# First norm of a two-layer graph kernel: its positive part made from a second, feature-major layout of x instead of by transposes

## Reference, cut to what matters

```python
h = maximum(layernorm(x), 0)
W = zeros(1024, 1024).at[src, dst].add(edge_weight)      # edge weights scattered into a dense matrix
x = x + h @ W.T + bias
h = maximum(layernorm(x), 0)
for layer in (0, 1):                                      # two graph layers with weights Ws, Wn of 1024 x 1024
    agg = segment_sum(h[src], dst) / degree
    h = h @ Ws + agg @ Wn + b                             # relu after layer 0
x = x + h
```

## Time and profile before

| | us |
|---|---|
| median of 3 runs | 824.98 (823.58 to 825.27) |
| the profiled execution, own time | 826.84 |
| its span | 825.1 |
| TensorE (PE) matmul busy in it | 798.2 (97%) |
| VectorE (DVE) busy | 469.8 (57%) |
| GpSimd (POOL) busy | 384.3 (47%) |
| ScalarE (ACT) busy | 378.3 (46%) |
| mean granted TensorE clock | 0.998 of full |

### The profile page before, as it was taken

The page is one execution under the profiler, slowest core; times in us unless marked ns, Lnnn a source line. Parts: engine busy times, 40 slices in busy tenths (PEclk is TensorE's granted clock), DMA queues, the critical chain, the costliest instruction groups (busy, mean ns, idle before and its releaser), DMA issues.

```text
span 825.1 us, 13564 instructions
## 1 busy us (share of the span) xinstructions
PE 798.2 (97%) x4660; PEld 647.1 (78%) x4661; DVE 469.8 (57%) x799; ACT 378.3 (46%) x491; POOL 384.3 (47%) x558
## 2 busy tenths in 40 slices
PE   3999999999999999999999999999999999999998
PEld 2666788888888878887887878888877888878786
DVE  7999666657542677856623453232556757336443
ACT  6755653443354222222336876543222333257653
POOL 3000056556735688756661210114788676724311
PEclk9999999999999999999999999999999999999999
DMA  3122335565464863556865653555753669758654
GB/s 108 43 69 82 99 116 177 172 182 170 159 234 159 275 207 105 181 202 216 319 219 180 196 175 102 179 175 178 268 170 116 196 212 332 253 180 281 209 170 138
DMA packets 82520, 148.57 MB, mean 180 GB/s; under 512 B 9973, under 2 KB 21356, under 8 KB 82448
## 3 DMA queue, kind: packets, MB, share of 16 engines
q1 hardware_dynamic: 62506, 102.68, 39.2%
q10 hardware_dynamic: 18422, 40.05, 13.7%
q0 software_dynamic: 1520, 4.92, 1.5%
HBM read 100.34 MB, written 47.27 MB: 179 GB/s over the span
## 4 chain that ended last, share of the span: by engine, by line
PE 73%; POOL 8%; issue 5%; DMA 4%; DVE 4%; ACT 4%; SPq 1%; ACTq 0%; POOLq 0%; DVEq 0%
PE bank L1306 28%; PE bank L1334 19%; PE bank L1243 13%; POOL T L848 3%; PE bank L1161 3%; PE bank L1150 3%; DMA stage<-hT_scratch 3%; PE bank L1166 2%; POOL T L846 2%; ACT split L1009 1%; PE bank L1145 1%; POOL S L817 1%; POOL S L813 1%; ACT Ax L1041 1%; PE bank L1350 1%
## 5 line engine op out<-in xcount | busy, mean ns | idle before, releaser
L1306 PE MATMUL bank<-slot,split 128*128 128x512 f32 x1680 | 388.6, 392 | 2.9 <-POOL split L831 1.2
L1306 PEld LDWEIGHTS bank<-slot,split 128*128 128x128 f32 x1680 | 314.5, 188 | 71.6 <-issue 3.0
L793 POOL TENSOR_TENSOR AT<-AT,az 128x50 int32 (+3 forms) x288 | 84.6, 294 | 141.3 <-DMA az<-asum_scratch 102.6
L831 POOL TENSOR_TENSOR split<-stage,split 128x512 fp32r<-128x512 f32 x50 | 64.5, 1292 | 141.3 <-ACT split L1009 141.3
L1612 DVE TENSOR_TENSOR slot<-T,slot 128x512 fp32r<-128x512 f32 x64 | 71.5, 1117 | 95.6 <-ACT slot L1000 91.1
L1041 ACT CAST Ax<-AT 128x1280 fp32r<-128x1280 uint16 x40 | 106.8, 2674 | 31.6 <-PE bank L1334 21.1
L1612 DVE TENSOR_TENSOR slot<-wst,slot 128x512 fp32r<-128x512 f32 x48 | 45.8, 980 | 84.8 <-ACT slot L1000 84.8
L1243 PE MATMUL bank<-slot,split_m 128*128 128x512 f32 x320 | 89.6, 394 | 0.0
L1000 ACT CAST slot<-T 128x512 fp32r<-128x512 f32 x64 | 40.0, 624 | 107.3 <-POOL T L848 80.6
L1334 PE MATMUL bank<-slot,Ax 128*128 128x512 f32 x320 | 77.2, 393 | 0.5 <-ACT Ax L1041 0.5
L1721 DVE SCALAR_TENSOR_TENSOR cst<-bank,dinv,stage 128x512 f32<-128x512 f32 x40 | 30.0, 751 | 73.9 <-PE bank L1334 73.4
(11 more groups left out here) (170 smaller groups left out, 1035.3 us busy)
## 6 DMA issues: line engine op xcount, KB each, us to landing
stage<-hT_scratch SPq DMA_DIRECT2D x90, 256.0 KB, 3.8
wst<-in_L_gnn_W_neigh SPq DMA_DIRECT2D x56, 256.0 KB, 4.0
wst<-in_L_gnn_W_self SPq DMA_DIRECT2D x56, 256.0 KB, 3.2
x1b_scratch<-x ACTq DMA_DIRECT2D x10, 512.0 KB, 5.0
hT_scratch<-hTs ACTq DMA_DIRECT2D x10, 512.0 KB, 3.2
stage<-prod0s_scratch SPq DMA_DIRECT2D x20, 256.0 KB, 2.9
hT_scratch<-h1s ACTq DMA_DIRECT2D x20, 256.0 KB, 3.5
stage<-prod1s_scratch SPq DMA_DIRECT2D x20, 256.0 KB, 2.8
```

Source lines behind the costliest of these rows:

```text
L793: pool.tensor_tensor(a, a, az32[:, n % NZ, pairs * pos:pairs * (pos + 1)], ALU.add) \
L831: pool.tensor_tensor(split[:, v % 2, 1, :], source(v), split[:, v % 2, 0, :].bitcast(F32), ALU.subtract).then_inc(s_olo, 1)
L1306: last = pe.matmul(dense_bank(v, which)[:, :], split[:, v % 2, a, NT * k:NT * (k + 1)], slot[t % 2][:, b, HF * (HK * which + k):HF * (HK * ...
```

## The change

x is given to the kernel a second time as `x_cols`: for each row tile the transpose, features on partitions, 4 KB per partition. For tiles 2 to 9 the transposed relu(x - mean) is made from it:
- a DMA of 512 KB per tile puts the columns in `xh` (two buffers in place of h0's). SP issues those of tiles 2 and 3 behind the az loads of the start, ScalarE the other six;
- ScalarE writes `mean` = identity times -mean (128x128) in place of the 128x1024 relu; TensorE multiplies it by a matrix of ones, which puts the row of -mean on all partitions. The product stands in M(i - 2) behind block 5 of 8 (for tile 2 behind M(0));
- VectorE adds it to the columns (`columns_less_mean`, PSUM against SBUF, in place);
- ScalarE takes the relu as the high part, one operation from SBUF; VectorE takes max(xh, 0) - high as the low part, one operation with both inputs in SBUF.

The order becomes A(i+2), M(i), T0(i+2), T1(i-1), B(i). On VectorE the low part of tile i + 1 and `block_lo(i - 2)` now stand at M(i), behind A(i+2); before, `block_lo(i - 1)` stood at T1(i - 1), ahead of the low part. The operand loads of products 0 and 1 wait for the low parts of tiles 8 and 9 in place of the last transposes. Tiles 0 and 1 keep their transposes.

```diff
--- before.py
+++ after.py
@@
+MEAN_AT = 5
@@ -200,6 +201,7 @@
         hTs = sb("hTs", [P, 2, KT * NT], F32, mixing)
+        all_ones = sb("all_ones", [NT, P], F32, mixing)
         mixing.close()
@@ -218,8 +220,9 @@
         split_m = sb("split_m", [P, 2, 2, KT * NT], F32R, mixing)
-        h0 = sb("h0", [NT, 2, F], F32, mixing)
+        xh = sb("xh", [P, 2, F], F32, mixing)
         xt = sb("xt", [NT, NX - 1, F], F32, mixing)
+        mean = sb("mean", [NT, 2, NT], F32, mixing)
         mixing.close()
@@ -255,6 +258,10 @@
         s_x = [sem(f"s_xin{i}") for i in range(NX)]
+        s_xc = [sem(f"s_xcols{i}") for i in range(2)]
+        s_ones = sem("s_ones")
+        s_mean = sem("s_mean")
+        s_sub = sem("s_sub")
         s_vec = sem("s_vec")
@@ -464,9 +471,19 @@
 
-        def h0_banks(i):
-
-            return 6 if i <= 1 else 4
+        def mean_bank(i):
+            return bank[4][:, NT * (i % 2):NT * (i % 2 + 1)]
+
+        def by_chunk(i):
+            return xh[:, i % 2, :].rearrange("p (k n) -> p k n", k=KT)
+
+        def load_columns(eng, i):
+            n = rows_of(i)
+            eng.dma_start(by_chunk(i)[:, :, 0:n], x_cols[NT * F * i:NT * F * i + n * F]
+                          .rearrange("(p k n) -> p k n", p=P, k=KT)).then_inc(s_xc[i % 2], 16)
+
+        def columns_loaded(i):
+            return 16 * (i // 2)
 
@@ -614,7 +631,7 @@
                 else:
-                    sp.wait_ge(s_t0, TN)
+                    sp.wait_ge(s_lom, TN - 1 + v)
                 if v >= VL and p == 2:
@@ -675,6 +692,9 @@
                 load_asum(n)
+            for i in range(2, 4):
+                sp.wait_ge(s_t0, i - 1)
+                load_columns(sp, i)
             sp.wait_ge(s_wt, 2 * KT)
@@ -888,24 +908,29 @@
                 act.wait_ge(s_x[i], 16)
-                act.activation(h0[:, i, :], xt[:, i, :], ACT.Copy, accum_out=total_x[:, i, 0:1]).then_inc(s_sumx, 1)
+                act.activation(xh[:, i, :], xt[:, i, :], ACT.Copy, accum_out=total_x[:, i, 0:1]).then_inc(s_sumx, 1)
                 act.wait_ge(s_sumx, 3 * i + 1)
...
                 act.wait_ge(s_sumx, 3 * i + 2)
-                act.activation(h0[:, i, :], xt[:, i, :], ACT.Square, bias=less[:, 0, i:i + 1],
+                act.activation(xh[:, i, :], xt[:, i, :], ACT.Square, bias=less[:, 0, i:i + 1],
                                accum_out=total_x[:, i, 1:2]).then_inc(s_sumx, 1)
...
             def above_mean(i):
-                if i >= 2:
-                    act.wait_ge(s_less, i - 1)
+                act.activation(xh[:, i, :], x_tile(i), ACT.Relu, bias=less[:, 0, i:i + 1]).then_inc(s_h0, 1)
+
+            def columns_and_mean(i):
+                if i >= 4:
+                    act.wait_ge(s_lom, i - 1)
+                    load_columns(act, i)
                     act.wait_ge(s_t0, i - 1)
-                act.activation(h0[:, i % 2, :], x_tile(i), ACT.Relu, bias=less[:, 0, i:i + 1]).then_inc(s_h0, 1)
+                act.wait_ge(s_less, i - 1)
+                act.activation(mean[:, i % 2, :], ident[:, :], ACT.Copy, scale=less[:, 0, i:i + 1]).then_inc(s_mean, 1)
 
@@ -915,12 +940,14 @@
             def h0_hi(i):
+                if i >= 2:
+                    act.wait_ge(s_sub, i - 1)
+                    act.wait_ge(s_mm, i - 1)
+                    act.activation(split_m[:, i % 2, 0, :], xh[:, i % 2, :], ACT.Relu).then_inc(s_hi, 1)
+                    return
                 act.wait_ge(s_t0, i + 1)
-                if i >= 2:
-                    act.wait_ge(s_mm, i - 1)
                 for b in range(2):
-                    last = act.activation(split_m[:, i % 2, 0, TC * b:TC * (b + 1)],
-                                          bank[h0_banks(i) + b][:, 0:TC], ACT.Copy)
+                    last = act.activation(split_m[:, i % 2, 0, TC * b:TC * (b + 1)], bank[6 + b][:, 0:TC], ACT.Copy)
                 last.then_inc(s_hi, 1)
@@ -968,7 +995,7 @@
                 if j == TURN_STATS + 2:
-                    above_mean(2)
+                    columns_and_mean(2)
                     root_of(0, 2)
@@ -1010,7 +1037,7 @@
                 if what == "A":
-                    above_mean(i)
+                    columns_and_mean(i)
                     root_of(0, i)
@@ -1171,7 +1198,13 @@
                     pe.wait_ge(s_lom, i)
-                turn_tile(h0[:, i % 2, :], h0_banks(i)).then_inc(s_t0, 1)
+                turn_tile(xh[:, i, :], 6).then_inc(s_t0, 1)
+
+            def spread_mean(i):
+                pe.wait_ge(s_mean, i - 1)
+                if i >= 4:
+                    pe.wait_ge(s_sub, i - 3)
+                pe.matmul(mean_bank(i), all_ones[:, :], mean[:, i % 2, :], start=True, stop=True).then_inc(s_t0, 1)
 
@@ -1262,6 +1295,8 @@
             first_mix_step(KT - 1).then_inc(s_mm, 1)
+            pe.wait_ge(s_ones, 1)
+            spread_mean(2)
 
@@ -1270,15 +1305,15 @@
             for what, i in mix_order()[EARLY_STEPS:]:
-                if what == "T0":
-                    turn_h0(i)
-                elif what == "M" and i >= 1:
+                if what == "M" and i >= 1:
                     pe.wait_ge(s_hi, i + 1)
...
                         last = mix_step(i, k)
+                        if k == MEAN_AT and i + 2 < TN:
+                            spread_mean(i + 2)
                     last.then_inc(s_mm, 1)
@@ -1480,12 +1515,23 @@
 
+            def columns_less_mean(i):
+                dve.wait_ge(s_xc[i % 2], columns_loaded(i))
+                dve.wait_ge(s_t0, i + 1)
+                dve.tensor_tensor(by_chunk(i), by_chunk(i), mean_bank(i).unsqueeze(1).to_broadcast([P, KT, NT]),
+                                  ALU.add).then_inc(s_sub, 1)
+
             def h0_lo(i):
                 dve.wait_ge(s_hi, i + 1)
+                if i >= 2:
+                    dve.scalar_tensor_tensor(out=split_m[:, i % 2, 1, :], in0=xh[:, i % 2, :], scalar=0.0,
+                                             in1=split_m[:, i % 2, 0, :].bitcast(F32), op0=ALU.max,
+                                             op1=ALU.subtract).then_inc(s_lom, 1)
+                    return
                 for b in range(2):
                     part = slice(TC * b, TC * (b + 1))
-                    last = dve.tensor_tensor(split_m[:, i % 2, 1, part], bank[h0_banks(i) + b][:, 0:TC],
-                                             split_m[:, i % 2, 0, part].bitcast(F32), ALU.subtract)
+                    last = dve.tensor_tensor(split_m[:, i, 1, part], bank[6 + b][:, 0:TC],
+                                             split_m[:, i, 0, part].bitcast(F32), ALU.subtract)
                 last.then_inc(s_lom, 1)
@@ -1603,6 +1649,7 @@
             h0_lo(1)
+            dve.memset(all_ones[:, :], 1.0).then_inc(s_ones, 1)
 
@@ -1614,13 +1661,19 @@
                     mix_A(i)
+                elif what == "M":
+                    if 2 <= i + 1 < TN:
+                        h0_lo(i + 1)
+                    if i >= 2:
+                        block_lo(i - 2)
                 elif what == "T0":
-                    h0_lo(i)
+                    columns_less_mean(i)
                     inverse_std(0, i)
...
                         dve.wait_ge(s_vec, 16)
-                    dve.wait_ge(s_h0, i + 1)
+                    if i < 2:
+                        dve.wait_ge(s_h0, i + 1)
                     link(dve.tensor_tensor(x_tile(i), x_tile(i), bias[:, :], ALU.add))
@@ -1637,10 +1690,6 @@
                                              in1=rstd[:, 1, i:i + 1], op0=ALU.mult, op1=ALU.mult).then_inc(s_norm, 1)
-                elif what == "T1":
-                    if i < WB:
-                        block_lo(i)
-
 
@@ -1761,14 +1810,14 @@
         ahead = i + 2 < TN
-        steps += [("A", i + 2)] * ahead + [("M", i)] + [("T1", i - 1)] * (i >= 1)
-        steps += [("T0", i + 2)] * ahead + [("B", i)]
+        steps += [("A", i + 2)] * ahead + [("M", i)] + [("T0", i + 2)] * ahead
+        steps += [("T1", i - 1)] * (i >= 1) + [("B", i)]
     return steps
...
 
-_INS = ["x", "dst", "src_cols", "dst_cols", "weight_cols", "L0_gnn_bias", "L1_gnn_W_self0", "L1_gnn_W_neigh0",
+_INS = ["x", "x_cols", "dst", "src_cols", "dst_cols", "weight_cols", "L0_gnn_bias", "L1_gnn_W_self0", "L1_gnn_W_neigh0",
         "L1_gnn_b0", "L1_gnn_W_self1", "L1_gnn_W_neigh1", "L1_gnn_b1"]
@@ -1781,6 +1830,8 @@
         laid[name] = np.asarray(inputs[v]).reshape(NG * GC, EP).T
+    tiles = [np.asarray(inputs["x"])[NT * i:min(NT * (i + 1), N)] for i in range(TN)]
+    laid["x_cols"] = np.concatenate([t.T.reshape(KT, P, len(t)).transpose(1, 0, 2).reshape(-1) for t in tiles])
     arrays, args = {}, []
...
         a = np.ascontiguousarray(laid[name])
```

(2 more changed lines are left out.)

## The result

The changed kernel takes **828.25 us** (median of 5 runs, 827.47 to 830.12), the kernel before 824.42 on the same chip (5 runs, 823.58 to 825.27). The ratio is 1.0049 [1.0033, 1.0065]: slower by 3.8 us. The prediction was 830.1, its range of 8 in 10 826.6 to 833.6. The profiled execution had an own time of 828.25 and a span of 826.5, against 826.84 and 825.1 before.

What follows compares the result with a forecast made beforehand. TensorE looked the bound, but at product 0 POOL was level to 0.2 us. Product 0 +3.5 and clock +1.6 make +5.1: 831.9 profiled, median 830.1; own range 828.6 to 832.5, 8 in 10 826.6 to 833.6.

Steps and rivals of the forecast that it cites:

- no loss of clock: Rival: product 0 starts 3.5 us later but no time is lost at 1.2 GHz: 828.5; 12 in 100.
- a low part that doesn't stop POOL: Rival: VectorE's new low part leaves POOL's adds alone, SP's delay stays, +1.4 at product 0: 828.0; 12 in 100.
- The place: At product 0: TensorE ready 4.3 us earlier, at 228.6, but POOL's late operand starts it at 236.4, idle 7.8.
- The mean product: On TensorE in each mixing round: 0.27 us per product, a round of 12.04, and one wait of 0.5 in M(1).
- SP's queue: `block_lo(2)` and (3) come 2.9 and 3.6 us later, delaying SP's az units: +3.6 for POOL at add 134.
- POOL's adds: From add 134: +3.6 from SP, +4.0 low parts, +0.9 bias add, -2.5 swallowed wait; +6.0, adds end at 235.0.
- The clock: At product 0, after 7.8 us of TensorE idleness: one loss of 1.6 us at 1.2 GHz; bounds none and 3.3.
- Nothing takes the shift up: After product 0 TensorE runs without a gap from 232.9 to 283.6, so the delay reaches the end whole: 0 recovered.
- The baseline: The first profiled execution, 826.84 us, was 1.9 above the median, so the forecast was set from 824.98.
- The columns: DMA loads of the x columns land 4.0 us after issue, level with the round, costing nothing.
- late-columns rival: Rival: columns land in 5.0, every round loses 1.0, POOL passes on about 1: 831.2 to 832; 1 in 10.
- the prediction's ring: Loop from column load through VectorE's steps and relu of hn to the next load: 8.0 plus landing, 12.0 with 4.0.

Runs made afterwards that it cites:

- e10: The changed kernel measured once more with no edit: 830.02 us beside 824.77 for the kernel before, ratio 1.0069.
- e5: Changed kernel with SP's loads of weight blocks 4 to 7 one slot later and MIX_ADDS 20 in place of 23: 820.71 us, ratio 0.9959.
- e6: Kernel before with SP's block loads one slot later and MIX_ADDS 20 in place of 23: 824.46 us, ratio 1.0002.
- e3: Changed kernel with SP's loads of weight blocks 4 to 7 one slot later, behind the az units: 829.77 us, ratio 1.0059.
- e2: Changed kernel with the low part's second input from PSUM instead of SBUF, leaving out the true low part: 828.53 us, ratio 1.0046.
- e1: The kernel before run once more with no edit, for a second profile: 824.74 us, ratio 1.0002.
- e8: Changed kernel with ScalarE's store of x1 issued behind the relu of hn instead of ahead of it: 827.83 us, ratio 1.0035.
- e7: Changed kernel with 34 unread matmuls keeping TensorE busy through the idle stretch ahead of product 0: 827.74 us, ratio 1.0046.
- e9: Kernel before with product 0 held back by 27 matmuls on TensorE: 829.46 us, ratio 1.0067.
- e4: Changed kernel with MIX_ADDS 20 in place of 23, moving 30 of POOL's 270 adds behind operand_lo(0): 824.63 us, ratio 1.0003.

## Why the prediction was right, and where a term was not

**The number.** 828.25 lies in the range of 8 in 10, but just below the forecast's own range (828.6 to 832.5), and next to two rivals: no loss of clock (828.5) and a low part that doesn't stop POOL (828.0). The traces rule both out, by the clock of 0.50 in product 0 and by the adds of 1.32. e10's 830.02 is at the forecast. (By the chances stated, the range of 8 in 10 holds 87 in 100.)

**The place: right.** TensorE's saving stops at product 0, which POOL sets. Predicted for the end of the transposes 228.6, for the adds 235.0, for product 0 236.4, for the idle stretch 7.8; measured 228.81 (228.65 when the transposes are counted as 0.87 long, as the prediction did), 235.28, 236.71 and 7.90. e5 and e6 show it from the other side: with SP's delay and 30 of POOL's adds out of the way the change wins.

**The mean product: right.** The round was put at 12.04, and L1207 comes at 165.09, 177.14 and 189.19, every 12.05; so the product adds 0.28, where 0.27 was taken. (Its records' 3.2 us over eight products overlap their neighbours.) Its wait in M(1), 0.5 predicted, is 0.55.

**SP's queue: right.** `block_lo(0)` to (3) were put at 140.2, 152.2, 164.3 and 176.3, and end at 139.97, 152.11, 164.18 and 176.09; the unit of add 134 was put at 167.4, and POOL goes on at 167.54. But the +3.6 was not SP's alone: e3 took SP's waits away and add 134 came only 1.2 earlier.

**POOL's adds: right sum, wrong terms.** The low part does stop POOL, by 1.0 an add (1.32 against 0.27). It was counted four times, +4.0; but two of the four began while POOL was loading registers and held up only the next add, by 0.5 each (0.76 and 0.78 against 0.29), so it cost 2.9. The bias add of tile 9 fell into the adds as forecast, at 220.68; but the bias adds stopped more adds in other rounds too, +2.2 in all, where +0.9 was taken, and `block_lo` stopped fewer, -1.4, which had no term. The long register loads, 1.3 more than before from add 134 on, had none either. All this counts what each add takes over 0.29, by the VectorE operation beside it. The sum of the steps is +3.8 - 2.5 + 2.9 + 2.2 - 1.4 + 1.3 = +6.3, and the adds end 6.2 later (235.28 against 229.03); predicted +6.0. That the wrong terms offset each other is luck. The Trainium skill, "SBUF — State Buffer", section "Who interferes with whom", says that a VectorE instruction with two SBUF inputs blocks a GpSimd instruction that reads SBUF; these traces agree, 1.32 with both inputs in SBUF and 0.26 with one in PSUM (e2).

**The clock: right kind, a size that varies.** One loss of 1.6 was taken; it is 2.6 in the first profile (8.27 against 5.69 in e1) and 1.6 in e10 (7.29). With e2, e3 and e8, idle stretches of 5.85 to 8.32 cost product 0 1.3 to 2.6, and the longest not the most. The product it was taken from, 7.34, ran with a smaller part at 1.2 GHz (mean clock 0.77; here (0.50 x 5.5 + 1.00 x 2.8) / 8.3 = 0.67). The Trainium skill, "TensorE: Matmul & The Clock Gate", section "What's actually happening", says that the clock goes to 1.2 GHz after idleness; the 0.50 at 232.00 and e7's 1.00 agree.

**"Nothing takes the shift up": the step that failed.** TensorE ran on without a gap up to 283.6, but not behind it. e1's wait of 0.76 for `degs` ahead of product 10 does take 0.86 up. In the profiles the shift goes from 6.20 at product 1 to 3.8 at the end of the span, that is 2.4 less. Of this 0.86 has a place. e9, with the same kind of shift, lost 0.87 at that place and nearly nothing behind it; e10 still waits 0.49 for `degs` there, lost 0.26, and goes from 5.91 to 4.7 by the end. e6, a kernel before whose product 1 comes 0.42 after e1's, ends 1.8 after it. So about 1.4 of such shifts is scatter from execution to execution, and I take the other 1.5 for that; no run shows it as more. By the steps: +3.6 at product 0, +2.6 of clock, -2.4 = +3.8 measured, where +3.5, +1.6 and 0 = +5.1 was predicted. Two sizes were off in opposite directions, and the forecast came as near as it did partly for that.

**The baseline: a small error.** The sum was set against the first profile, in which a product lost 1.65 and a gap took 1.57, where e1 has 0.76 and no loss. It was put right through the median (826.84 to 824.98), so the forecast didn't suffer; but the row on the clock came from that one execution.

**The columns: a miss without effect.** Landing 5.4, not 4.0; the late-columns rival had its condition fulfilled and yet no price. By the prediction's ring, 8.0 and 5.4, a round would be 13.4; but the six loads of ScalarE are issued every 12.0 (136.6 to 196.6), so the 8.0 was too long, and no delay adds up from tile to tile.

## What to carry to other kernels

Before a saving on the busiest engine is counted, look at the first place behind it where that engine waits for another, and at how much room the other has: here 0.2 us at product 0 against a saving of 4.2. A change that lightens one engine by giving work to the others needs their queues cleared in the same step (e5: both SP's loads and POOL's adds), and it should be tested with them cleared before it is thrown away. Idleness made just ahead of a dense stretch costs the first product twice, once as the wait and once as the clock (1.3 to 2.6 here); how much of the second reaches the end of the program was within the scatter (e7).

## What the runs showed of the hardware that was not expected

POOL's load of 16 values from SBUF into registers takes 1.05 us, and often 1.8 to 3.9 when it begins near ScalarE's burst of 512 KB DMA issues (0.55 us before to 3.15 after the issue of the x1 store, in all runs but e8, where three lie outside); above the normal time it costs 2.8 us in the kernel before, 7.8 in the changed one, 10.7 in e2, 5.0 in e5. Whether the cause is the issue itself, the descriptors' traffic or SBUF reads of the stores was not tried and stays open.

VectorE's scalar_tensor_tensor (1.21 us) stops POOL as the plain tensor_tensor of the bias add does (an add of 1.32, and of 1.16 in the earlier trace rows), and no longer does with one input in PSUM (0.26).

After 7.90 of idleness product 0 ran 5.5 us at 1.2 GHz before the clock was granted in full, and after 8.32 (e10) 3.4. After 2.38 (e4) it ran at full clock.
